# Sixteen-head attention loop: the mix of a key tile in two halves of 256 queries

## What is computed

```python
def _L1_attn_ref(x, w_qkv, w_out):
    import jax, jax.numpy as jnp
    import numpy as np
    B, S, E, H = (2, 256, 128, 16)
    D = E // H
    b, s, e = x.shape
    qkv = jnp.einsum('bse,ef->bsf', x, w_qkv)
    qkv = qkv.reshape(b, s, 3, H, D).transpose(2, 0, 3, 1, 4)
    q, k, v = (qkv[0], qkv[1], qkv[2])
    scale = 1.0 / np.sqrt(D).astype(np.float32)
    scores = jnp.einsum('bhsd,bhtd->bhst', q, k) * scale
    attn = jax.nn.softmax(scores, axis=-1)
    out = jnp.einsum('bhst,bhtd->bhsd', attn, v)
    out = out.transpose(0, 2, 1, 3).reshape(b, s, e)
    return jnp.einsum('bse,ef->bsf', out, w_out)
```

## Time and profile before

| | us |
|---|---|
| median of three runs | 1060.2 (1058.15 to 1062.98) |
| the profiled execution | 1063.73 |
| its span, first to last instruction | 1061.9 |
| TensorE busy | 975.9 (92%) |
| VectorE busy | 808.6 (76%) |
| ScalarE busy | 705.1 (66%) |
| GpSimd busy | 277.1 (26%) |

### The profile page before, as it was taken

How to read it: one execution, slowest core, us unless ns; L and a number is a source line. 1 busy time by engine, 2 the same in 40 slices (tenths; PEclk the granted TensorE clock), 3 DMA queues, 4 the chain that set the end, 5 groups by cost and what they waited for, 6 DMA issues and landing times. The chain is left out here.

```text
span 1061.9 us, 18838 instructions
## 1 busy us (share of the span) xinstructions
PE 975.9 (92%) x6760; PEld 537.2 (51%) x6760; DVE 808.6 (76%) x1369; ACT 705.1 (66%) x1355; POOL 277.1 (26%) x288
## 2 busy tenths in 40 slices
PE   5499998899999999789889999999999899999997
PEld 3256686466666666442123222222222477888885
DVE  8968656467755855577878999999994478777877
ACT  6323458555544675324787888888887797888885
POOL 1137532526545545123212200000100013112201
PEclk9599999899999999888989999999999999999999
DMA  5000005796955856503001100000200103311111
GB/s 107 1 2 2 31 8 222 224 298 199 238 153 167 241 150 164 127 19 109 17 16 46 60 17 16 21 26 17 22 1 2 41 1 133 108 60 60 40 40 40
DMA packets 56580, 86.16 MB, mean 81 GB/s; under 512 B 15136, under 2 KB 33192, under 8 KB 55464
## 3 DMA queue, kind: packets, MB, share of 16 engines
q1 hardware_dynamic: 52088, 78.66, 25.2%
q0 software_dynamic: 3968, 6.10, 2.6%
q10 hardware_dynamic: 432, 0.20, 0.1%
HBM read 63.76 MB, written 21.43 MB: 80 GB/s over the span
## 5 line engine op out<-in xcount | busy, mean ns | idle before, releaser
L2421 ACT ACTIVATE narrow_att_probs<-psum 128x512 f32<-128x512 f32 x512 | 264.7, 604 | 73.6 <-PE psum L2341 73.2
L2468 DVE TENSOR_REDUCE front_maxima<-psum 128x1 f32<-128x1024 f32 x240 | 282.1, 1219 | 23.7 <-PE psum L1190 19.1
L2341 PE MATMUL psum<-narrow_att_q,narrow_att_k 50*128 50x512 bf16 x448 | 146.2, 384 | 5.6 <-ACT narrow_att_probs L2421 4.7
L1190 PE MATMUL psum<-narrow_att_k,narrow_att_q 48*128 48x512 bf16 x448 | 133.4, 386 | 13.3 <-DVE front_maxima L2468 5.4
L2354 PE MATMUL psum<-narrow_att_probs,narrow_att_v_ones 128*32 128x512 f32 x1024 | 138.8, 615 | 0.1
L2951 DVE TENSOR_TENSOR moe_hidden_lo<-moe_hidden,moe_hidden_hi 128x512 fp32r<-128x512 f32 x144 | 104.4, 751 | 38.9 <-ACT moe_hidden_hi L2853 38.3
L2849 ACT ACTIVATE moe_hidden<-psum,back_up_bias 128x512 f32<-128x512 f32 x144 | 96.3, 690 | 32.8 <-PE psum L73 32.8
L2039 DVE TENSOR_REDUCE gated_nmax<-psum 128x1 f32<-128x1024 f32 x62 | 73.0, 1220 | 50.4 <-PE psum L1709 50.1
L1784 ACT ACTIVATE lead_room<-psum 128x512 f32<-128x512 f32 x62 | 33.8, 595 | 101.8 <-PE psum L1658 101.7
L1190 PEld LDWEIGHTS psum<-narrow_att_k,narrow_att_q 48*128 48x128 bf16 x448 | 25.7, 95 | 148.5 <-DVE front_maxima L2468 131.2
L1561 POOL DMA_INDIRECT home_rows<-gated_y,gated_to_row x62 | 62.0, 1000 | 133.2 <-ACT gated_y L1779 123.5
(11 more groups left out here) (458 smaller groups left out, 1876.5 us busy)
## 6 DMA issues: line engine op xcount, KB each, us to landing
gated_k_ring<-gated_k_dram SPq DMA_DIRECT2D x62, 288.0 KB, 4.7
lead_room<-gated_v_dram SPq DMA_DIRECT2D x32, 256.0 KB
moe_mixb<-moe_mix_scratch SPq DMA_DIRECT2D x8, 1024.0 KB, 4.8
gated_k_dram<-gated_keys SPq DMA_DIRECT2D x8, 512.0 KB, 5.7
gated_v_dram<-gated_v_stage SPq DMA_DIRECT2D x2, 2048.0 KB, 8.4
lead_wqk_hi<-gated_v_dram SPq DMA_DIRECT2D x16, 256.0 KB
lead_wqk_lo<-gated_v_dram SPq DMA_DIRECT2D x14, 256.0 KB
gated_q_dram<-lead_room SPq DMA_DIRECT2D x8, 256.0 KB, 2.3
```

What stands on the lines that cost most here:

```text
L1190: return pe.matmul(out, self.stack(0, n // 2)[64 * a:64 * a + self.ROWS, n % 2, r, tile(qt)], self.stack(1, n // 2)[64 * a:64 * a + self.R ...
L2341: pe.matmul(psum[:, SCORE_BANK + j % 3, :], ks(n // 2, kt // QT, e)[rows, tile(kt % QT)], qs(n // 2, n % 2, e)[rows, :], start=True, stop= ...
L2421: act.activation(probs[:, k % 3, 2 * e + u % 2, :], psum[:, SCORE_BANK + j % 3, :], ACT.Exp, scale=SCALE).then_inc(exped, 1)
L2468: dve.tensor_reduce(maxima[:, n % 2, at:at + 1], chunk.rearrange("p a b -> p (a b)"), AX.X, ALU.max).then_inc(chunk_used, 1)
```

## The change

The mix of a key tile is made in two halves: half 0 takes the first 256 queries (columns of `probs` and of the bank), half 1 the other 256. Within an odd unit, half 0 stands behind the first score and half 1 behind the second, where before the whole mix stood behind the second. Both halves wait for the same exponentials; half 0 of a half's first key tile waits for the copied sums; half 1 alone counts up `mixed`. The last mix of all, behind the loop, is made as two halves in a row.

```diff
-                def mix(n, kt):
+                def mix(n, kt, half):
 
                     pe.wait_ge(exped, (n * STILES + kt + 1) * G)
-                    if kt == 0:
+                    cols = slice(half * BANK // 2, (half + 1) * BANK // 2)
+                    if kt == half == 0:
                         if n % 2 == 0:
                             pe.wait_ge(v_ready, n // 2 + 1)
                         if n >= 1:
                             pe.wait_ge(sums_copied, n)
                     for j in range(G):
-                        last = pe.matmul(psum[32 * j:32 * j + 32, SUM_BANK, :], v_ones[:, n // 2 % 2, kt, j, :],
-                                         probs[:, (n * STILES + kt) % 3, j, :],
-                                         start=(kt == 0), stop=(kt == STILES - 1), skip_group_check=True)
-                    last.then_inc(mixed, 1)
+                        last = pe.matmul(psum[32 * j:32 * j + 32, SUM_BANK, cols], v_ones[:, n // 2 % 2, kt, j, :],
+                                         probs[:, (n * STILES + kt) % 3, j, cols],
+                                         start=(kt == half == 0), stop=(kt == STILES - 1 and half == 1), skip_group_check=True)
+                    if half == 1:
+                        last.then_inc(mixed, 1)
...
                             score(n, u, x)
-                        k = n * UNITS + u - 3
-                        if u % 2 == 1 and k >= 0:
-                            mix(k // UNITS, k % UNITS // 2)
+                            k = n * UNITS + u - 3
+                            if u % 2 == 1 and k >= 0:
+                                mix(k // UNITS, k % UNITS // 2, x)
...
-                mix(HALVES - 1, STILES - 1)
+                for x in range(2):
+                    mix(HALVES - 1, STILES - 1, x)
```

## The result

The changed kernel takes 1077.15 us (median of four runs, 1075.87 to 1080.35) against 1060.02 for the kernel before (now four runs, 1058.15 to 1062.98). The ratio is 1.0169, with a 95% interval of 1.0138 to 1.0200: slower by 17 us. The profiled execution took 1076.58 us, its span is 1074.8.

The account below looks back on a forecast made before the run. The prediction took the ring score, exponential, fourth score, mix (2.40 us) as the bound. Terms 10.8 + 1.1 + 3.4 + 1.5 - 1.0 = +15.8 us took the profiled 1063.7 to 1079.5, scaled to 1076 us; range 1063 to 1088.

Parts of the forecast that it names:

- the second ring: Odd unit's first maximum matmul, half 0, second maximum, VectorE's reduction, next tile's first: from 1.91 to 2.58 us, becoming the bound.
- The bound before: Sixteen-head loop before the change: bound by score, exponential, fourth score and mix at 2.40 us a tile, not by VectorE.
- ScalarE's ring: Chain from score to exponential to fourth score to mix and the next tile's score, 2.40 us before the change.
- Half a mix, 0.57 us: On TensorE, from the start of half a mix to the next maximum: 0.57 us, bounds 0.43 and 0.68.
- rivals 1 and 2: Half a mix costs 0.68 us, total 1093 us, chance 0.12; or only 0.43 us, total 1058 us, chance 0.05.
- A half, +1.20 us: Eight tiles in the loop's regular part: 6 x 0.18 + 0.13 - 0.01 = 1.20 us more, nine of them +10.8.
- The early part: Loop's 37 tiles from 494.24 to 605.41: +3.4 us for 19 regular tiles, +1.5 for 15 longer ones.
- the 15 long tiles: Tiles before 605.41 lengthened by a turn, front projection chunk or 1.2 GHz clock: 0.1 us each, together +1.5.
- The rest to the last turn: From 788.26 on: seven tiles to 805.24 add 1.1 us, the tiles without maxima behind them give -1.0.
- the five tiles: Loop's end, without maxima, bound by ScalarE: each falls from 2.39 to 2.00 us, together -2.0.
- Rival 3: The odd unit's first maximum is released early enough, TensorE alone binds at 2.22 us a tile; 1039 us, chance 0.04.
- Rival 4: Other chains set each half's pace, so only part of the 0.18 us per regular tile shows; 1064 us, chance 0.05.

Follow-up runs that it names:

- short reduction: VectorE's maximum reduction reads only the first of a chunk's two banks; ratio to the kernel before 0.9846 in the changed kernel, 0.9939 in the kernel before.
- the last experiment: Changed kernel with half 0 behind the even unit's second score and half 1 behind the odd unit's fourth matmul; 1077.02 us, ratio to the kernel before 0.9931.

## Why the prediction was right

The forecast of 1076 us, slower by the second ring, came out at 1077.15. Step by step:

- *The bound before.* Not VectorE: shown by the short reduction in the kernel before, whose half changes by 0.11 us only. ScalarE's ring: its parts sum to the tile, and with half of the mix taken out of it and the other ring kept short (one half behind each unit) 2.40 fell to 2.22.
- *Half a mix, 0.57 us.* Measured 656.61 to 657.18: 0.57. The interpolation between 128 and 512 columns held, and rivals 1 and 2, which changed this price, fell.
- *The second ring, 2.58 us.* Measured 2.60: 0.32 + 0.57 + 0.42 + 1.22 + 0.06 with the parts not rounded (the last one was 0.05 in the forecast). VectorE's idle time in a tile is 0.24 us where I had some 0.3. The ring's parts were shown one by one: the place (whole mix behind the third score, 3.03), the slope (128, 256, 384 columns) and VectorE's share (short reduction).
- *A half, +1.20 us.* Measured 21.65 - 20.32 = 1.33, the difference being for the most part the 0.02 in each of seven tiles; nine halves gave +12.0 where the sum had +10.8.
- *The early part, +4.9 us by the forecast.* Measured +3.4 with the granted clock 0.04 above that of before, and +6.0 with clocks alike. The forecast had set no term for a clock that differs between the two kernels. I had set 0.1 for each of the 15 long tiles, with 0 to 0.3 as bounds; what each gave was not taken apart.
- *The rest to the last turn.* The forecast had +1.1 for the seven tiles to 805 and -1.0 for the tiles without maxima, together +0.1; measured +0.4. Here a step was incomplete: I had each of the five tiles fall to 2.00 us. They alternate between 1.99 and 2.33, since S2 waits for the exponential of the S3 before, and I had compared ScalarE's four exponentials with the tile, 1.92 against 2.00, but not followed the last of them to the bank that it frees. Counted from mix to mix, two tiles fell to 2.33 only, 0.66 more than the sum had. Against that, two tiles fell by 0.40 that the sum didn't have falling (one from 2.39 to 1.99, one from 2.98 to 2.58), and the last mix of all came 0.40 later behind the one before it. So +0.1 against +0.4 is partly luck too.
- *Rival 3, that M2 is released early enough*, fell: M2 waits for VectorE in each regular tile. Its size was right all the same. With the path from M3 to the next M2 shortened by 0.53 us (short reduction), TensorE alone binds, at 2.21 to 2.22 us a tile, where I had put 2.22.
- *Rival 4, hidden tiles*, fell: all regular tiles show the whole 0.20.

The sum for the profiled execution was +15.8 us, and the loop grew by 15.8; the early part's miss (-1.5), the nine halves' miss (+1.2) and the rest (+0.3) cancelled, so the agreement to the tenth is luck. On chip 14, with clocks alike, the loop grew by 18.4, 2.6 more than the sum. That the loss lies within some 3 us of the sum rests on the ring, whose half repeated to 0.01 us. The medians differ by 17.1, the two profiled executions by 12.9, because the stages ahead of the loop ended 3.0 us earlier in one of them.

## What to carry to other kernels

When a loop is bound by a ring of three engines, write down each ring with its sum, the ones that don't bind too. A piece of work that is moved into idle time on the critical ring may stand, by its place, inside another ring, and that one's slack is the real budget: 0.49 us here (2.40 - 1.91), while half 0 put 0.67 into it. Put such a piece between chunks of a buffer pair, not between the two writes that complete one chunk; on the same chip the same two halves, one behind each unit, made the loop 8.1 us shorter where the change made it 18.4 longer.

## What the runs showed of the hardware that I had not expected

- Splitting a block of fp32 matmuls in four column groups into two blocks of half the columns costs nothing where they stand together: 16 records of 256 columns hold TensorE 1.00 us, like 8 of 512, and a half takes 20.35 us against 20.32.
- Apart, each block pays at both of its ends: 0.32 us from the last bf16 matmul to the block instead of 0.22, and 0.57 us to the next bf16 matmul, of which two passes of 256 columns stream 0.43. That is 0.24 us for a block, and it is what the second block adds to TensorE's own work in the last experiment: 3 x 0.22 + 0.32 + 1.00 = 1.98 us with one block, 2.22 with two. I have called this the turn of the array; whether it comes from the other layout in column groups or from the change between bf16 and fp32, no run separates.
- The kernel before took 17.9 us longer ahead of this loop in the execution on chip 14 than in that of the result, and the same time within 0.3 us in the loop (342.6 and 342.9).
- The changed kernel's irregular part took 115.4 us at a granted clock of 0.99 and 118.2 at 0.96, the kernel before 112.0 and 112.2 at 0.95: the clock that a stretch gets can differ between two executions of one kernel, and with it the difference of two kernels.
